# Splitting one semaphore for the first weights and biases, and loading the later tokens ahead of the values' bias

## The reference, cut to what matters

```python
x = x + attn(layernorm(x), Wq, bq, Wk, bk, Wv, bv, Wo, bo)   # x: 1 x 2048 x 512
x = x + ffn(layernorm(x), gate_w, expert_w, expert_b)

def attn(x, ...):
    Q = (x @ Wq + bq)   # 32 heads of 16
    K = (x @ Wk + bk)   # 8 heads of 16, each used by 4 query heads
    V = (x @ Wv + bv)
    out = softmax(Q K^T / 4) V
    return out @ Wo + bo

def ffn(x, ...):
    logits = x @ gate_w.T                 # 8 experts
    top 2 of 8, softmax over the two
    out = sum of the two chosen (x @ expert_w[e].T + expert_b[e]), weighted
```

## Time and profile before

| | |
|---|---|
| median of 3 executions | 1713.09 us (1711.37 to 1714.03) |
| the profiled execution's own time | 1721.97 us |
| its span on the core | 1720.0 us |
| its mean granted TensorE clock | 0.98 of full speed |
| PE, DVE, ACT, POOL busy | 95%, 83%, 75%, 33% of the span |
| first matmul of a transpose | 10.69 us |
| first matmul of a projection | 17.55 us |
| first matmul of the maxima | 76.83 us |

### The profile page before, as it was taken

One profiled execution on the slowest core, in us unless ns is written; L12 is line 12 of the kernel. 1 busy time (PEld: TensorE's weight loads), 2 busy tenths in 40 slices (PEclk: granted clock), 3 DMA queues, 4 the chain that ended last, 5 costly groups with the idle time before them and its releaser, 6 DMA issues.

```text
span 1720.0 us, 38278 instructions
## 1 busy us (share of the span) xinstructions
PE 1635.6 (95%) x13793; PEld 796.8 (46%) x13794; DVE 1424.0 (83%) x1694; ACT 1287.4 (75%) x2417; POOL 565.8 (33%) x828
## 2 busy tenths in 40 slices
PE   6999999999999999999999999999999999876994
PEld 3533444444444444444444444444444445655883
DVE  4388999999999999999999999999999941545455
ACT  3226888888888888888888888888888897333552
POOL 3121243333333333333333333333333445333221
PEclk9999999999999999999999999999999999978997
DMA  7435344423343333233323333322321142754467
GB/s 205 111 104 118 71 104 112 85 67 91 75 91 71 91 75 77 67 91 86 69 67 91 73 81 84 98 67 67 91 67 36 42 139 70 282 198 137 148 210 255
DMA packets 86838, 179.03 MB, mean 104 GB/s; under 512 B 20206, under 2 KB 24318, under 8 KB 85936
## 3 DMA queue, kind: packets, MB, share of 16 engines
q1 hardware_dynamic: 49312, 85.12, 21.0%
q0 software_dynamic: 34656, 88.26, 16.4%
q10 hardware_dynamic: 2736, 3.67, 0.6%
HBM read 91.14 MB, written 86.23 MB: 103 GB/s over the span
## 4 chain that ended last, share of the span: by engine, by line
PE 89%; DMA 3%; issue 2%; ACT 2%; POOL 2%; DVE 1%; another core or an unknown queue 1%; SPq 1%; ACTq 0%; POOLq 0%; DVEq 0%
PE bank L1034 33%; PE bank L995 25%; PE bank L1024 15%; PE bank L1120 6%; PE bank L965 5%; PE bank L1166 2%; ACT o_acc L815 1%; PE bank L1212 1%; PE bank L986 1%; DMA x_all<-in_L_attn_x 1%; PE bank L1226 1%; DMA o_acc<-y_rows 1%; DMA sums<-o_acc 0%; PE bank L1005 0%
## 5 line engine op out<-in xcount | busy, mean ns | idle before, releaser
L1312 DVE TENSOR_REDUCE max_kc<-bank 128x1 f32<-128x1024 f32 x1024 | 1243.4, 1222 | 65.7 <-PE bank L995 48.1
L838 ACT ACTIVATE arena_p<-bank 128x512 f32<-128x512 f32 x2048 | 1110.4, 595 | 160.0 <-PE bank L1024 121.4
L1034 PE MATMUL bank<-arena_p,v_cur 128*32 128x256 f32 x8192 | 653.5, 391 | 10.5 <-ACT o_acc L815 10.5
L995 PE MATMUL bank<-k_st,q_st 48*128 48x512 f32 x2048 | 511.4, 496 | 0.8 <-ACT qf L785 0.8
L1024 PE MATMUL bank<-q_st,k_st 50*128 50x512 f32 x2048 | 441.7, 405 | 0.8 <-ACT arena_p L838 0.8
L995 PEld LDWEIGHTS bank<-k_st,q_st 48*128 48x128 f32 x2048 | 190.5, 183 | 428.3 <-issue 398.7
L1024 PEld LDWEIGHTS bank<-q_st,k_st 50*128 50x128 f32 x2048 | 294.8, 185 | 32.9 <-ACT arena_p L838 21.8
L1034 PEld LDWEIGHTS bank<-arena_p,v_cur 128*32 128x32 f32 x8192 | 162.4, 108 | 297.5 <-issue 154.0
L483 POOL DMA_DIRECT2D sums<-o_acc x128 | 64.9, 514 | 341.8 <-ACT o_acc L815 336.7
L965 PE MATMUL bank<-xT,arena_p 128*128 128x512 f32 x160 | 85.0, 645 | 5.4 <-DMA arena_p<-in_L_attn_bv 3.3
L486 POOL DMA_DIRECT2D sums_rec<-sums x32 | 18.3, 571 | 211.2 <-DVE sums L1342 211.2
(11 more groups left out here) (193 smaller groups left out, 999.9 us busy)
## 6 DMA issues: line engine op xcount, KB each, us to landing
slots_x<-pad_row POOLq DMA_DIRECT2D x27, 1295.0 KB, 6.1
q_st<-q_parts SPq DMA_DIRECT2D x192, 128.0 KB, 4.5
xs<-slots_x SPq DMA_DIRECT2D x39, 259.0 KB
q_parts<-parts SPq DMA_DIRECT2D x16, 512.0 KB, 3.3
we_raw<-in_L_ffn_expert_w POOLq DMA_DIRECT2D x8, 1024.0 KB, 6.3
at_parts<-o_hl POOLq DMA_DIRECT2D x128, 64.0 KB, 2.3
we_his<-o_hl POOLq DMA_DIRECT2D x32, 256.0 KB, 2.4
we_hi<-we_his SPq DMA_DIRECT2D x8, 1024.0 KB
```

The costliest lines, as they stand in the source:

```text
L838: act.activation(probs[:, u % PRING, :], bank[:, ring_bank(("score", u)), :], ACT.Exp, scale=SCALE).then_inc(p_ready, 1)
L995: return pe.matmul(bank[:, 2 + 2 * (m % 2) + q, :], q_st[r:r + CROW, j % SLOTS, h, qt * P:(qt + 1) * P], k_st[r:r + CROW, key_slot(j // NC ...
L1034: mm = pe.matmul(bank[32 * h:32 * h + 32, 6, half], v_cur[:, kt, :], probs[:, (REP * kt + h) % PRING, half], start=(kt == 0 and part == 0) ...
L1312: dve.reduce_max(max_kc[:, m:m + 1], bank[:, 2 + 2 * (m % 2):4 + 2 * (m % 2), :].rearrange("p a s -> p (a s)"), AX.X).then_inc(m_done, 1)
```

## The change

The one semaphore `wa_dma` is replaced by five: one for each first weight (`wk_dma`, `wq_dma`, `wv_dma`), one for `bk` and `bq` together (`b_dma`), one for the four copies of `bv` (`bv_dma`). Each consumer waits for what it reads:

- PE waits for `Wk` before the first projection, for `Wq` before the second, for `Wv` before the values.
- ACT waits for `bk` and `bq` before `deviation(1)`.
- DVE waits for `bv` before `evacuate_values`.
- SP waits for `Wk` and `Wq`, then issues the tokens of chunks 1 to 3, and only after them the four copies of `bv`; the relay of the landings to `x_ready` stands behind these four issues.

```diff
-        wa_dma = sem("wa_dma")
+        wk_dma = sem("wk_dma")
+        wq_dma = sem("wq_dma")
+        wv_dma = sem("wv_dma")
+        b_dma = sem("b_dma")
+        bv_dma = sem("bv_dma")
...
-            sp.dma_start(bk_sb[:, :], bk).then_inc(wa_dma, 16)
-            sp.dma_start(bq_sb[:, :], bq).then_inc(wa_dma, 16)
-            for t in range(TT):
-                sp.dma_start(bv_sb[:, t, :], bv.partition_broadcast(P)).then_inc(wa_dma, 16)
-            sp.wait_ge(wa_dma, 16 * 9)
+            sp.dma_start(bk_sb[:, :], bk).then_inc(b_dma, 16)
+            sp.dma_start(bq_sb[:, :], bq).then_inc(b_dma, 16)
+            sp.wait_ge(wk_dma, 16)
+            sp.wait_ge(wq_dma, 16)
             for c in range(1, NC):
                 sp.dma_start(x_all[:, c * TT:(c + 1) * TT, :], x_t[:, c * TT:(c + 1) * TT, :]).then_inc(x_dma[c], 16)
+            for t in range(TT):
+                sp.dma_start(bv_sb[:, t, :], bv.partition_broadcast(P)).then_inc(bv_dma, 16)
             for c in range(1, NC):
                 sp.wait_ge(x_dma[c], 16)
                 sp.sem_inc(x_ready, 1)
...
-            act.dma_start(wk_sb[:, :, :], Wk.rearrange("(k p) n -> p k n", p=P)).then_inc(wa_dma, 16)
-            act.dma_start(wq_sb[:, :, :], Wq.rearrange("(k p) n -> p k n", p=P)).then_inc(wa_dma, 16)
-            act.dma_start(wv_sb[:, :, :], Wv.rearrange("(k p) n -> p k n", p=P)).then_inc(wa_dma, 16)
+            act.dma_start(wk_sb[:, :, :], Wk.rearrange("(k p) n -> p k n", p=P)).then_inc(wk_dma, 16)
+            act.dma_start(wq_sb[:, :, :], Wq.rearrange("(k p) n -> p k n", p=P)).then_inc(wq_dma, 16)
+            act.dma_start(wv_sb[:, :, :], Wv.rearrange("(k p) n -> p k n", p=P)).then_inc(wv_dma, 16)
...
             evacuate_transposes(0)
-            act.wait_ge(wa_dma, 16 * 9)
+            act.wait_ge(b_dma, 32)
             deviation(1)
...
                 transpose_chunk(c)
                 if c == 0:
-                    pe.wait_ge(wa_dma, 16 * 9)
+                    pe.wait_ge(wk_dma, 16)
                 pe.wait_ge(t_evac, 2 + TT * (c + 1))
                 for k in range(KD):
                     projection_step(0 if c == 0 else 4 + c, k)
                 if c == 0:
+                    pe.wait_ge(wq_dma, 16)
                     for p in range(1, 5):
...
             pe.wait_ge(proj_evac, 5)
+            pe.wait_ge(wv_dma, 16)
...
+            dve.wait_ge(bv_dma, 16 * TT)
             for c in range(NC):
                 evacuate_values(c)
```

## The result

The changed kernel took 1703.03 us (median of 5 runs, 1702.11 to 1704.24) against 1711.37 for the kernel before (5 runs, 1710.03 to 1714.03). The ratio is 0.9948, with a 95% interval from 0.9933 to 0.9962: 8.3 us less, where 4.2 were forecast. The sign was right and the size was off by a factor of two.

A forecast was written before the change was run, and what follows sets the result against it. The prediction took PE, busy 95% of the span, as the bound. An earlier start (-2.6 us) and no half clock (-1.6) made -4.2, from 1713.1 to 1708.9 us, 0.25% less; the range was 1706.0 to 1712.0.

The forecast's parts named there:

- What bounds the kernel: PE is busy 95% of the span; a gain at its first projection, at 17.55, should be carried to the end.
- Part 1, the start: PE's first projection starts at 14.92 instead of 17.55, after the evacuated transposes: 2.63 us gained, between 2.4 and 2.7.
- Part 2, the clock: No half clock at PE's first forty projection records: 17.4 us rather than 18.96, 1.6 less, bounds 0 to 1.7.
- Part 3, what is late next: SP's relay of chunk 1 comes at 18.5 and may go to 22.4 before anything is lost.
- The slower rival: SP's relay of chunk 1 held until `bv` passes the queue; at 31 it is +4.4, 1717.5 us; chance 0.07.
- Part 4, the added waits: New waits on DVE, PE and ACT and the extra semaphores cost 0, between -0.1 and 0.2 us.
- The sum: Start and clock, -2.6 - 1.6 = -4.2 us over the whole kernel, set against the median: 1713.1 to 1708.9 us.

The follow-up runs named there:

- bias_first: The changed kernel with the four loads of `bv` issued ahead of SP's wait for the weights, as before: 1705.48 us, ratio 0.9981 to the kernel before.
- split_only: The changed kernel with SP's old order, tokens of chunks 1 to 3 waiting for all nine loads: 1721.20 us, ratio 0.9991 to the kernel before.
- split_again: A repeat, on chip E, of the changed kernel with split semaphores but SP's old order: 1720.44 us, ratio 0.9982 to the kernel before.
- gaps_filled: The changed kernel with small unread products in PE's short pauses at the transposes of chunks 1 to 3: 1717.15 us, ratio 0.9972 to the kernel before.
- waits_and_names: The kernel before with four unused semaphores and four more waits that are already met when reached: 1721.61 us, ratio 0.9995 to the kernel before.
- before_again: The kernel before, unchanged, timed and profiled once more on chip A: 1723.23 us, ratio 1.0000.
- before_third: The kernel before, unchanged, timed and profiled again on chip C: 1722.43 us, ratio 1.0000.
- after_again: The changed kernel, unchanged, repeated beside the kernel before on chip B: 1705.42 us, ratio 0.9976.
- after_fourth: The changed kernel, unchanged, repeated beside the kernel before on chip D: 1706.95 us, ratio 0.9973.
- before_fourth: The kernel before, unchanged, timed and profiled again on chip D: 1710.45 us, ratio 1.0000.

## Why the prediction was off, step by step

**What bounds the kernel.** Right. What moves PE in the first 80 us moves the end: `start_held`, with PE's start put back and all else changed, is back at the time of before (1.0006), and its values start at 62.39 where the four profiles of before have a mean of 62.5.

**Part 1, the start.** The mechanism is shown in all five profiles of the change: it starts 0.78 us after the transposes, released by ACT. The term was mis-sized. The forecast took 2.63 from one profile in which `bv` had landed at 17.50. The four profiles of the kernel before start at 17.55, 18.83, 18.47 and 18.50, mean 18.3. The five of the change start at 15.38, 15.25, 14.94, 14.93 and 14.49, mean 15.0. The transposes themselves start between 10.15 and 10.80 in these nine; counted from them the difference is 3.3 as well. The row used was the earliest of four, and the bounds "between 2.4 and 2.7" were those of a single execution.

**Part 2, the clock.** For the change the term is right in kind and was a little small. The forty take 17.40 or 17.41 in all five profiles, for 18.96 to 19.79 before (mean 19.4): 2.0 instead of 1.6. The two terms together give 5.3, and so do the first transposes of chunk 1, which start at 37.54 before and at 32.24 after, by the same means.

The rule that was weighed against the change here (the Trainium skill, "TensorE: Matmul & The Clock Gate", section "Part 4: PE-mode transpose") would have PE reach the projection with a cold array. Five profiles of the change and `bias_first` say otherwise; `split_only`, `split_again` and `gaps_filled` agree with it, behind the same transposes and the same pause of 0.78 us. What decides between them was not found: of nine profiles, three began low. So the prediction's reason, that a pause of about 0.7 keeps the full clock, is not a safe one, and that all five profiles of the change began high may be in part luck.

**Part 3, what is late next.** The conclusion holds (no row of PE waits for the relay). Two of its numbers were wrong and cancelled: the tokens went out at 14.38 instead of 11.6, since `Wq` lands 9.4 us after its issue and not 6.5, and the four issues of `bv` took 2.60 and not 5.36. So SP was free at 18.51, as forecast, by luck. The relay came at 19.66, when chunk 1 had landed (5.2 us after its issue), and not when SP was free. The slower rival's long hold of SP's queue was not seen. The DMA issues of the changed kernel, 0:80 (KB each, us from issue to landing), against the earlier trace rows:

```profile
arena_p<-in_L_attn_Wq ACTq DMA_DIRECT2D x1, 1024.0 KB, 9.4
```

The 6.5 of before was no landing that the trace had seen by itself: nine loads counted up one semaphore, and which of them a count belongs to is inferred. The five profiles with the shared semaphore that have no extra waits give 6.0 to 7.0 (`waits_and_names` 7.8); the ten with one for each load give 7.6 to 10.5. How much of the difference is the inference and how much a later landing, no run here separates. The mistake cost nothing, since `Wq` is wanted only by the fifth step, at 15.38 + 8 x 0.43 = 18.8, and had landed at 14.35.

**Part 4, the added waits.** No cost was seen: `waits_and_names` stands at 0.9995, with no change inside the interval.

**The sum: the step that failed.** It set -4.2, worked out in one profiled execution, against a median of three runs, on the ground that the work of the edited stage is the same in both. From that median, 1713.09, down to the measured 1703.03 are 10.1 us. They come apart as follows.

First, 4.2 us are the forecast, and 1.7 are its base: with two more runs the median of before is 1711.37.

Second, both terms were too small. By the means of four profiles and five they are 3.3 and 2.0, together -5.3. On to the first product of the attention weights with the values (151.55 before, 145.60 after, by the same means) it is -5.95. The 0.6 in between are no term of the prediction: the one later projection at half clock is 0.3 us longer before (5.65 against 5.36), and in `before_again` and `before_third` PE waits 0.5 and 1.0 us longer than elsewhere ahead of the last transposes. There ACT's evacuation stands behind a store, as in `before_third`:

```profile
54.43 0.69 ACT L785 ACTIVATE qf<-bank,bk_sb 128x512 f32<-128x512 f32 x1 [4.63 <-DMA k_parts<-parts]
...
56.41 1.13 PE L955 MATMUL bank<-ident,arena_p 128*128 128x128 f32 x8 [2.17 <-ACT xT L776]
```

This longer pause is in three of the eight profiles with the late tokens (`split_only` is the third, with 0.5) and, by more than 0.1, in none of the eight with the early ones, so the earlier tokens may be worth a few tenths of a microsecond. With -5.3 or -5.95 for the -4.2 and 1711.37 as the base, the sum would have come to 1706.1 or 1705.4, which leaves 2.4 to 3.0 us of the 8.3 without a term.

The timed pairs bear the sum out. What was then timed in four comparisons, each on one chip (B to E), is 0.9976, 0.9973, 0.9973 and 0.9970, which times the kernel before is -4.1, -4.7, -4.6 and -5.2 us. The forecast's ratio, 0.9975, lies inside all four intervals, and so do those of -5.3 and -5.95, about 0.9969 and 0.9965. So where both kernels ran on one chip in larger groups, the forecast was right to within 1 us.

Third, the profiled execution and the timed runs of the kernel before were not the same thing. That execution ended 8.9 us above the median, which the prediction put aside. This did not move its number, since it added up a difference inside the first stage, but it shows how far an execution and a median can lie apart. Who waited for whom, over its whole span, shows a releaser that no line of the kernel gives:

```profile
ACT ys L908 <- remote: 7.0, 2, 4.0
ACT o_acc L861 <- remote: 6.0, 1, 6.0
ACT x2T_hi L849 <- remote: 5.7, 1, 5.7
```

They stand on the chain of waits of the same execution, behind 1490 us, in the last stage that the change does not touch:

```profile
1495.95 3.33 another core or an unknown queue
...
1514.92 6.57 another core or an unknown queue
```

The chain of `after_third`, a profile of the changed kernel on chip C, has the same:

```profile
1489.04 4.46 another core or an unknown queue
...
1507.68 6.81 another core or an unknown queue
```

The first profile of the change, `after_again`, `after_fourth`, `before_fourth` and `bias_first` have none. From the first product of the attention weights with the values to the end it takes 1568.9 to 1571.4 us with them in the kernel before and 1567.9 and 1572.7 in the changed one; without them it takes 1557.2 before and 1556.0 to 1558.0 after. So either kernel occurs with and without them, and profiles with them are about 13 us longer in this part. That is nearly all of the 14 us behind the edited stage that the two profiles of the result seemed to show. They go with the chip and not with the kernel: every profile of chips A, C and E has them, and none of B and D. In a difference of profiles they would have passed for an effect of the change.

**What stays open.** In the first comparison the change was 8.3 us faster, in the four others 4.1 to 5.2. One number on record bears on the rest: the mean granted clock of each run. The five runs of the change in the first comparison all stand at 0.987 or 0.988. On chip B the twelve runs of the change part by this number: five at 0.988 or 0.989 have a mean of 1703.1 us, seven at 0.982 to 0.985 one of 1707.1. The kernel before parts in the same way, into thirteen at 0.988 or 0.989 (1707.7 us) and ten at 0.981 to 0.986 (1711.5 us). Like against like the change is worth 4.6 and 4.4 us there (4.7 and 3.3 on chip D, parted at the same place); on chip B the upper group of the change against the lower group of before would give 8.4. So five runs that all fall into the upper group, against a mixed or a lower five, can make up the missing 3 us. Whether that happened is not shown, since the clocks of the five runs of before are not on record. The runs of before come from two occasions, three shown ahead of the prediction (1711.37 to 1714.03) and two more (1710.03 and 1710.99), and the levels of the two chips without the unnamed waits differ by 2.9 us too (1708.19 and 1711.09). Also open are what the unnamed waits are, what puts a run into the one group or the other, and why the projection starts at half clock in some executions with the same pause.

## What to carry to other kernels

A semaphore that counts many loads makes everyone wait for the slowest, and the price is the pause plus the clock that the pause costs: here 3.3 and 2.0 us for four small bias copies that PE never needed. Take a term from several executions, for here one was off by a fifth. If a profiled execution lies 9 us off the median, find the waits that make the difference. Compare runs on one chip, in groups large enough to hold what a kernel scatters between by itself: five runs against five were 3 us off here. A landing time on a shared semaphore is an inference; here the same load read up to 4 us later once it had its own.

## What the runs showed of the hardware

- Waits without a named releaser in the last stage, with the same instructions: in all profiles from three of the chips (medians of before 1722.7 to 1723.6) and in none from two (1708.2 and 1711.1). With them this part of the program is about 13 us longer. The first comparison's own profiled execution of before had them; its timed runs (1710.03 to 1714.03) lie at the level of the chips without.
- Two groups of runs of the same kernel on one chip, 4 us apart, with mean granted clocks of 0.988 to 0.989 and 0.981 to 0.986 (chip B: 1703.1 and 1707.1 us for the change, 1707.7 and 1711.5 for before).
- The granted-clock column stands at 1.00 in a stretch whose weight loads take 0.34 us instead of 0.19 (`split_only`, to 19.6; `before_again` too, where the column of `before` shows 0.50). In this stage the durations told the clock, and the column did not always.
- The eight records of a later projection still ran at half clock once in each of the five profiles of the change (5.3 to 5.4 us, at about 51), after a pause of 0.69 like its neighbours'. It was not there (3.70 three times) in `gaps_filled`, with the pauses filled, nor in `start_held`, with the pauses as they were.
- The four issues of the same 64 KB bias copies took 2.60 us behind 3 MB of tokens and 5.35 ahead of them (`split_only`), the opposite of what the slower rival feared. In `before` one of the four took 2.89 us, with a median of 0.79 for the four; why is not shown.
